# Fused attention and feed-forward layers on one core: the filling products on TensorE taken out

## The reference, cut to what matters

```python
x = x + attn_a(layernorm(x), W1, b1, Wp, bp)            # causal, 1024 keys
x = x + ffn(layernorm(x), w_gate, w_up, w_down)
x = x + attn_b(layernorm(x), Wq, Wk, Wv, Wo, last_k_init, last_v_init)   # window of 64
x = x + ffn(layernorm(x), w_gate, w_up, w_down)

def ffn(x, w_gate, w_up, w_down):
    gate = einsum('bsd,hd->bsh', x, w_gate / 127)
    up = einsum('bsd,hd->bsh', x, w_up / 127)
    return einsum('bsh,dh->bsd', silu(gate) * up, w_down / 127)
```

## Time and profile before

| | us |
|---|---|
| median of 3 runs | 1201.09 |
| lowest and highest | 1200.05, 1207.57 |
| the profiled execution's own time | 1202.65 |
| its span, first to last instruction | 1200.9 |
| TensorE busy in the span | 1096.6 (91%) |
| VectorE busy | 810.4 (67%) |
| ScalarE busy | 739.7 (62%) |
| GpSimd busy | 381.3 (32%) |
| mean granted TensorE clock | 0.985 |

### The profile page before, as it was taken

One profiled execution on the slowest core, in us unless ns is written; L12 is line 12 of the kernel. 1 busy time (PEld: TensorE's weight loads), 2 busy tenths in 40 slices (PEclk: granted clock), 3 DMA queues, 4 the chain that ended last, 5 costly groups with the idle time before them and its releaser, 6 DMA issues.

```text
span 1200.9 us, 32268 instructions
## 1 busy us (share of the span) xinstructions
PE 1096.6 (91%) x13309; PEld 668.1 (56%) x13309; DVE 810.4 (67%) x1546; ACT 739.7 (62%) x1060; POOL 381.3 (32%) x385
## 2 busy tenths in 40 slices
PE   7878898999998889999999889999899898999997
PEld 5433247766773326766775234776686332477666
DVE  6798826756878853666797792675588778166552
ACT  5366783665556785476555778466646577746653
POOL 7632142123234314202324413222223332421242
PEclk9899999999999999999999999999999899999999
DMA  8610001041132000122223000103023100011201
GB/s 300 213 61 16 7 11 52 32 132 61 51 108 65 16 7 26 60 65 83 81 73 108 21 8 11 52 31 131 28 70 100 49 17 11 7 51 50 63 20 37
DMA packets 70385, 71.64 MB, mean 60 GB/s; under 512 B 26016, under 2 KB 62304, under 8 KB 69344
## 3 DMA queue, kind: packets, MB, share of 16 engines
q1 hardware_dynamic: 70240, 69.56, 17.6%
HBM read 23.60 MB, written 8.39 MB: 27 GB/s over the span
## 4 chain that ended last, share of the span: by engine, by line
PE 65%; DVE 16%; ACT 7%; issue 5%; DMA 3%; POOL 3%; SPq 0%; POOLq 0%; ACTq 0%; DVEq 0%
PE ring L1715 11%; PE ring L1747 8%; PE ring L1748 7%; PE ring L1682 6%; DVE peak L1269 5%; PE ring L1637 5%; ACT probs_causal L1470 4%; PE ring L1761 4%; PE ring L1766 3%; DVE peak_c L1269 3%; PE ring L1587 3%; DVE xn L1162 2%; PE ring L1589 2%; PE ring L1588 2%; PE ring L1607 2%
## 5 line engine op out<-in xcount | busy, mean ns | idle before, releaser
L1470 ACT ACTIVATE probs_causal<-ring 128x1024 f32<-128x1024 f32 (+1 forms) x320 | 286.2, 941 | 130.8 <-PE ring L1682 76.8
L1269 DVE TENSOR_REDUCE peak<-ring 128x2 f32<-128x1024 f32 (+5 forms) x320 | 323.3, 1031 | 55.8 <-PE ring L1637 32.9
L1682 PE MATMUL ring<-q_st,k_st 64*64 64x192 f16 (+5 forms) x2752 | 168.1, 296 | 29.6 <-ACT probs_causal L1470 17.4
L1137 POOL TENSOR_TENSOR h_lo<-h_f,h_hi 128x512 fp32r<-128x512 f32 x96 | 122.1, 1289 | 181.8 <-ACT h_hi L1504 181.5
L1715 PE MATMUL ring<-probs_causal,V 128*32 128x512 f32 (+3 forms) x1536 | 165.8, 513 | 6.1 <-POOL probs_causal L1122 4.6
L1747 PE MATMUL ring<-xf_hi,w_gu_sb 128*128 128x512 f32 x384 | 159.3, 415 | 4.4 <-DVE xf_lo L1169 3.1
L1128 POOL TENSOR_TENSOR onf<-osb,onf 128x512 f32<-128x512 f32 x64 | 81.7, 1277 | 237.4 <-DVE onf L1312 236.9
L1122 POOL TENSOR_SCALAR_AFFINE_SELECT probs_causal<-probs_causal 128x512 f32<-128x512 f32 x128 | 80.7, 634 | 226.2 <-ACT probs_causal L1470 225.8
L1748 PE MATMUL ring<-xf_lo,w_gu_sb 128*128 128x512 f32 x384 | 151.6, 395 | 0.0
L1682 PEld LDWEIGHTS ring<-q_st,k_st 64*64 64x64 f16 x2752 | 67.5, 106 | 144.6 <-ACT probs_causal L1470 68.8
L1637 PE MATMUL ring<-k_st,q_st 64*64 64x512 f16 (+7 forms) x1536 | 123.8, 340 | 25.3 <-DVE peak L1269 16.3
(11 more groups left out here) (157 smaller groups left out, 1974.3 us busy)
## 6 DMA issues: line engine op xcount, KB each, us to landing
q_st<-q_part SPq DMA_DIRECT2D x96, 128.0 KB
w_qkv<-img_qkv SPq DMA_DIRECT2D x7, 1536.0 KB, 7.6
on_lo<-onf SPq DMA_DIRECT2D x64, 128.0 KB, 2.6
k_st<-k_part SPq DMA_DIRECT2D x48, 144.0 KB, 2.1
k_st<-k_part SPq DMA_DIRECT2D x48, 128.0 KB, 2.1
y<-X SPq DMA_DIRECT2D x8, 512.0 KB, 3.0
wp_sb<-img_wp SPq DMA_DIRECT2D x7, 512.0 KB, 3.6
x_next<-in_x SPq DMA_DIRECT2D x3, 1024.0 KB, 5.4
```

What stands on the lines that cost most here:

```text
L1137: pool.tensor_tensor(h_lo[m][:], h_f[m][:], h_hi[m][:].bitcast(F32), ALU.subtract).then_inc(h_lo_done, 1)
L1269: dve.tensor_reduce(dst, scores, AX.X, ALU.max).then_inc(a_max, 1)
L1470: act.activation(in_banks(block[0:rows, n % slots], unit, w), heads_of(flat_of(a, e), unit, w)[0:rows], ACT.Exp, scale=back[a % 2]).then_i ...
L1682: last = pe.matmul(psum[BLOCK * m:BLOCK * m + BLOCK, r, per * n:per * n + w], keys[rows_of(r), head, first_key + BLOCK * m:first_key + BLO ...
```

## The change

`keep_busy` and its call are taken out. The planner, its tables, the banks, the five products at the start and everything on the other engines stay.

```diff
-            def keep_busy(a, e):
-
-
-                if (a, e) in FILLED:
-                    bank, count = FILL[a, e]
-                    wait_for(FILLED[a, e])
-                    for n in range(count):
-                        pe.matmul(ring[:, bank, :].rearrange("p (h c) -> p h c", h=4), ident_b[:],
-                                  ident_b[:, None, :].to_broadcast([P, 4, P]), start=True, stop=True,
-                                  skip_group_check=True)
-
...
             def run(part, wide_weights=False):
                 for a, e, step in part:
                     kind = e[0]
-                    if kind != "U":
-                        keep_busy(a, e)
                     if kind == "U":
```

## The result

The changed kernel takes 1220.11 us (median of 6 runs, 1213.33 to 1224.10) against 1202.24 us for the kernel before (6 runs, 1200.05 to 1207.57). The ratio is 1.014, with a 95% interval of 1.0111 to 1.0168: slower, by 13 to 20 us. The profiled execution spans 1218.1 us against 1200.9, so it stands for the difference.

What follows compares the result with a forecast made beforehand. TensorE was taken to bound most of the span, waits for VectorE at stage boundaries the rest. Terms summed to 20.4 us, less 2.5 for escapes, forecast as +18 us: 1219 us, range 1202 to 1230.

Steps and rivals of the forecast that it cites:

- The products themselves: At all 29 places: removing 185 products, 40 us of TensorE's work, gains 0; upper bound 2.5 us at four first turns.
- The waits: keep_busy's waits for an idle bank's last reader, 2.9 us idle ahead of 11 fillings: gain 0, bound 2.9 us.
- The steps between layers: Eight layer steps: a clock fall at each, 1.60 us apiece less one existing, 11.2 us; two paying twice, 3.2 us.
- escapes: Some steps may keep the clock, as two of three did at 3.7 us: 2.5 us taken off the sum.
- The W places: Ahead of the first down product of six feed-forward halves: even chance of a clock fall at each, 3.6 us.
- Start and attention: One filling at the start, half a chance of a fall, 0.8 us; six in the attention, one more fall, 1.6 us.
- The price of half clock: In dense products and attention: half a microsecond lost per microsecond at half clock; 1.60 us for one stretch of 3.41 us.
- Few falls: Rival: four of the eight steps fall and none of the W places, +5 us, 1206 us; chance 0.18.
- no effect: Rival: all falls lie where fillers don't touch, as in the attention, so the time stays 1201 us; chance 0.07.
- fillers cost time: Rival: at four causal-to-sliding steps 2.5 us comes back, waits may add 1 or 2, giving 1197 us; chance 0.04.
- Falls that last twice as long: Rival: eight steps cost 3.4 us each and W places 3.4 at even chances, +34 us, 1235 us; chance 0.07.
- The sixteen transposes of a step: Sparse work at each unfilled layer step, 8.4 or 7.2 us; the prediction is wrong if the clock holds through it.

Runs made afterwards that it cites:

- e8_no_first_turn: Kernel before without the four fillings of seven ahead of the first turn at steps from causal to sliding layer: 1201.10 us, ratio 0.9986.
- e3_waits_only: Kernel before with the waits for idle banks' readers kept at all 29 places and the 185 products removed: 1217.57 us, ratio 1.0136.
- e2_turns_only: Kernel before with only the sixteen fillings at the steps between layers kept, 118 of 185 products: 1210.21 us, ratio 1.0075.
- e1_down_only: Kernel before with only the fillings ahead of the six down products kept, 48 of 185 products: 1210.40 us, ratio 1.0061.
- e9_no_small: Kernel before without the six fillings in the attention and the one at the start, 19 products: 1203.90 us, ratio 1.0003.
- e4_transposes: Kernel before with each filling product replaced by two float32 transposes of the identity at all 29 places: 1198.89 us, ratio 0.9973.

## Why the prediction was right

It said 1219 us with 1202 to 1230, and slower by over 1% at 0.65; measured were 1220.11 us and +1.4%. The mechanism came as told: the clock falls at the steps and at W, and the dense products behind run at half pitch. That the total came within 1 us is partly luck, since errors of its smaller terms met.

*The products themselves: 0.* Nothing speaks against it. e8_no_first_turn, the edit at the four places where time might have come back, shows none in its interval (up to 3.6 us are not excluded by it), and none place by place in its trace. Behind the fillers at the other places TensorE had idled anyway.

*The waits: 0.* Not told from 0 by e3_waits_only, to about 6 us; its falls are those of the change.

*The steps between layers: 11.2 + 3.2 us, less 2.5 for escapes.* All eight fell, six of them for 6.83 us, one for 10.24 and one for 3.41. The two profiled executions put them at 12.0 us; the medians, by e2_turns_only, at 7.8 (give or take 5). With the 14.4 us before escapes the prediction was 2.4 us above the profiled pair, and no step escaped; the 2.5 us taken off made that up. What a step costs follows from where its fall lies: at the first one the clock is low from 195.61 to 202.44, but the dense products only start at 198.08. That leaves 4.36 us of them at half clock, and the step cost 1.97 us, 0.45 for each. The sparse part shows no cost of its own, as the prediction had it.

*The W places: 3.6 us.* Too low: 5.9 us in the profiled executions, 9.5 (give or take 4.6) by e1_down_only. Five of six fell where an even chance had been given. And one row was taken for four: the prediction read L1733's 0.37 us of idle time at one W place as slack at all four that have a projection behind them. Only two of the four have it, as the view of waits of the kernel before and its timeline at the other one say:

```profile
PE ring L1733 <- POOL on_lo L1132: 1.3, 2, 0.9
...
1055.55 0.36 PE L1733 MATMUL ring<-wp_sb,on_hi 128*128 128x256 f32 x1 [0.94 <-POOL on_lo L1132]
```

At these two, a fall cost 1.0 us (the 1.0 that the prediction allowed) and 0.5; at the two others, where the chain went through W already, it cost 1.5, as in the last layer.

*Start and attention: 0.8 + 1.6 us.* e9_no_small measures 0.4 us, give or take 2.6, which does not exclude them. In the profiled execution of the change the clock did not fall at the start (in that of e3_waits_only it did, at 23.68 us), and the rest of the program came out 1.0 us shorter.

So the largest term was right in its trace, W was some 2 us too low, and the small places some 3 us too high.

*The price of half clock.* The prediction read 0.5 us lost for each microsecond at half clock from two pairs of twins. In dense products that holds nearly: five falls of 3.41 us at W cost 1.5 us each against e1_down_only, 0.43 for each microsecond. Over the whole change it is (1218.1 - 1200.9) / (100 - 36) = 0.27, since much of the new falls stands in sparse time. The kernel before itself lies between: over the 72 executions of it that were measured beside the experiments, the eight with a clock of 0.980 or less had a median of 1208.37 us and the thirteen with 0.987 or more 1199.17. With median clocks of 0.9785 and 0.987 that is 9.2 us for some 21 us more at half clock, 0.44 for each. Its spread of 1% goes with its falls.

*The rivals.* Few falls and no effect are out by the windows above. That fillers cost time found no support in e8_no_first_turn. Falls that last twice as long did come at the steps, but in the changed kernel they cost 2.4 us at most and not 3.4. The sixteen transposes of a step did not keep the clock; but that does not bear out the rule in the Trainium skill's "TensorE: Matmul & The Clock Gate" (Part 4: PE-mode transpose), by which transposes do not count as busy the same way. With float32 transposes as fillers the clock stayed at 1.00 at 13 of 14 places (e4_transposes), as with products; here the measurement decides against the rule.

## What to carry to other kernels

Idle time on TensorE is not free to leave empty. Where it stands ahead of a burst of dense matmuls, as the gaps of 3 to 8 us did here, products that nobody reads may pay for themselves, and what they pay can be read from the granted clock and the matmul pitch behind the gap. In this kernel fillings of 1.5 to 1.9 us did it, whether of products or of float32 transposes, and fillings of 0.6 us mostly did not.

To price a stall or a slow stretch, check its slack at each place where it will happen: one row showed 0.37 us of cover, and at two of the four places that it was read for there was none. Where two programs share an engine's list, compare the start of the same instruction in both; it gives the cost of each place from one execution each, finer than medians of whole runs can. And when a sum of terms comes out right, measure the terms one by one before trusting them.

## What the runs showed that I had not expected

Float32 transposes of an identity hold the clock as well as 512-column bfloat16 products do, at equal time filled (clock 0.984 and 0.985).

One filling in a step of 7 us was enough: with seven of the fifteen products gone (e8_no_first_turn) the clock stayed at 1.00 at all four steps. Two fillings did not always do: steps from sliding to causal layer fell with both in place, once in the kernel before (862.17) and three times in e9_no_small.

Falls are hard to drive out by filling more: the kernel with 86 more products had none at 138, 425 and 1005 us, where the kernel before had one each, but others at 266, 552 and 846 us in the sliding attention. There TensorE halts for 2 us and more in the middle of small products. One halt ends with a DMA; what causes those that the trace calls issue was not tried, and stays open.
